# A state-space stage on five engines: the steps at which its side work is called, and the pattern by which two engines share a product

## The reference, cut to what matters

```python
xz = x @ W_in.T                                  # x is normalised ahead of this
xc, z = jnp.split(xz, 2, axis=-1)                # 512 channels each
xc = silu(causal_conv(xc, conv_w) + conv_b)      # 4 taps along the tokens
dBC = xc @ W_x.T                                 # 64 + 16 + 16 columns
delta = softplus(dBC[..., :64] @ W_dt.T + b_dt)
deltaA = jnp.exp(delta[..., None] * A)           # a decay for each channel and state
BX = delta[..., None] * Bm[:, :, None, :] * xc[..., None]
# h[l] = deltaA[l] * h[l-1] + BX[l], along the tokens, 16 states a channel
y = jnp.einsum('bldn,bln->bld', hs, Cm) + Dp * xc
out = y * silu(z) @ W_out.T                      # then x + out
```

## Time and profile before

| | us |
|---|---|
| three timed runs | 1959.77, 1966.07, 2140.01 |
| their median | 1966.07 |
| the profiled execution | 1966.89 |
| its span in the trace | 1965.2 |
| GpSimd busy in the span | 1076.1 (55%) |
| VectorE busy in the span | 1325.1 (67%) |
| TensorE, ScalarE busy in the span | 1295.3 (66%), 905.4 (46%) |

### The profile page before, as it was taken

One profiled execution on the slowest core, in us unless ns is written; L12 is line 12 of the kernel. 1 busy time (PEld: TensorE's weight loads), 2 busy tenths in 40 slices (PEclk: granted clock), 3 DMA queues, 4 the chain that ended last, 5 costly groups with the idle time before them and its releaser, 6 DMA issues. The chain is left out here.

```text
span 1965.2 us, 33999 instructions
## 1 busy us (share of the span) xinstructions
PE 1295.3 (66%) x14068; PEld 616.3 (31%) x14068; DVE 1325.1 (67%) x1605; ACT 905.4 (46%) x1622; POOL 1076.1 (55%) x463
## 2 busy tenths in 40 slices
PE   5384948577584849444687736567766766648875
PEld 2121313132222214121233412344444444433433
DVE  3699899999999898998610053778669767525102
ACT  4566575747475665643322134446345544213220
POOL 1899999999999999998200011442344245330000
PEclk9687969788686969666798867678788877668988
DMA  4928183654728282740899741212331222139997
GB/s 116 216 56 202 41 205 78 161 129 98 192 55 219 50 193 54 184 107 0 313 411 421 327 129 33 55 30 50 67 72 34 62 56 68 46 103 367 418 421 271
DMA packets 193706, 300.07 MB, mean 153 GB/s; under 512 B 82704, under 2 KB 125200, under 8 KB 177168
## 3 DMA queue, kind: packets, MB, share of 16 engines
q1 hardware_dynamic: 188512, 295.17, 49.9%
q10 hardware_dynamic: 4688, 2.19, 0.4%
q0 software_dynamic: 352, 0.52, 0.1%
HBM read 255.37 MB, written 42.47 MB: 152 GB/s over the span
## 5 line engine op out<-in xcount | busy, mean ns | idle before, releaser
L376 POOL TENSOR_TENSOR state<-dx_rep,b_rep 128x2048 f32<-128x2048 f32 x128 | 578.8, 4526 | 52.1 <-issue 21.3
L608 DVE TENSOR_TENSOR_SCAN psum<-psum,state 128x1024 f32<-128x1024 f32 x160 | 365.2, 2283 | 27.7 <-POOL state L376 14.5
L744 PE MATMUL psum<-state,sel 128*32 128x512 f32 x1024 | 188.4, 833 | 269.1 <-POOL state L385 251.6
L491 ACT ACTIVATE psum<-delta_rep,a_neg 128x511 f32<-128x511 f32 x512 | 330.8, 679 | 60.5 <-DVE state L608 60.3
L608 DVE TENSOR_TENSOR_SCAN state<-psum,state 128x1024 f32<-128x1024 f32 x96 | 218.8, 2279 | 34.1 <-ACT psum L491 34.1
L385 POOL TENSOR_TENSOR state<-state,c_rep 128x1024 f32<-128x1024 f32 x96 | 226.0, 2354 | 0.0
L615 DVE TENSOR_TENSOR state<-psum,c_rep 128x1024 f32<-128x1024 f32 x160 | 195.9, 1225 | 5.5
L744 PEld LDWEIGHTS psum<-state,sel 128*32 128x32 f32 x1024 | 28.9, 129 | 398.8 <-issue 320.2
L668 PE MATMUL psum<-xt,w_in 128*128 128x512 f32 x256 | 128.1, 647 | 38.2 <-ACT z_silu L458 25.8
L488 ACT COPY psum<-zeros 128x2 f32<-128x2 f32 x160 | 25.9, 162 | 236.1 <-DVE state L615 226.5
L1855 PE MATMUL psum<-xt_delta,w_qkv 128*128 128x512 f32 x192 | 107.2, 697 | 12.4 <-DVE attn_t L1669 11.2
(11 more groups left out here) (222 smaller groups left out, 2449.2 us busy)
## 6 DMA issues: line engine op xcount, KB each, us to landing
moe_w_set<-in_w SPq DMA_DIRECT2D x30, 4096.0 KB, 33.0
delta_rep<-delta_scratch SPq DMA_DIRECT2D x128, 256.0 KB, 5.5
dx_rep<-dx_scratch SPq DMA_DIRECT2D x128, 256.0 KB, 8.1
b_rep<-bc_scratch SPq DMA_DIRECT2D x32, 256.0 KB, 4.8
delta_scratch<-delta SPq DMA_DIRECT2D x32, 256.0 KB, 7.8
c_rep<-bc_scratch SPq DMA_DIRECT2D x32, 256.0 KB, 7.9
moe_x<-x_after SPq DMA_DIRECT2D x16, 512.0 KB, 8.8
moe_w_set<-in_w SPq DMA_DIRECT2D x4, 2048.0 KB, 31.5
```

The costliest lines, as they stand in the source:

```text
L376: nc.gpsimd.tensor_tensor(ring[q % RING][:, :, :], dx_rep[u % CHUNKS][:, :, :], free_bcast(b_rep[q // QPB % 2][:, g, :], 1, CB), ALU.mult) ...
L491: ins = nc.scalar.activation(dec[:, i, 1:], delta_rep[u % CHUNKS][:, c, 1:], ACT.Exp, scale=a_neg[:, dt * CB + c, g:g + 1])
L608: nc.vector.tensor_tensor_scan(bx if by_pool(k) else flat, flat, bx, 0.0, ALU.mult, ALU.add).then_inc(S["scan_done"], 1)
L744: ins = nc.tensor.matmul(bank[32 * c:32 * c + 32, :], sel[:, :], ring[q % RING][:, c, :], start=False, stop=(g == NG4 - 1), skip_group_che ...
```

## The change

The step numbers are taken out of the loops into four tables, and some get other values. On ScalarE the copies of the transposes go from step 5 to 6, those of the first two convolutions from 13 to 12, the padded copies of tiles 2 and 3 from 15 to 14, and the second pair of `z_silu` from 29 to 30. On VectorE the gate goes from 4 to 5 (of every 8), the statistics from 20 to 18, the shift from 25 to 24; the addition of the output, both halves at step 9 before, is made at step 7 (first half) and 8 (second half). TensorE calls the convolution of tile 0 right after the projections of tiles 0 and 1, one quad earlier; the projection of tile 1 waits for the second half of the addition, that of tile 0 for the first half alone. On GpSimd `delta_x` of tiles 0 and 1 goes from after quad 14 to after quad 12; tiles 2 and 3 stay after quad 15. Of an item's 16 odd halves GpSimd leaves those of quads 6, 8, 12 and 15 to VectorE, where it left 3, 7, 11 and 15. The lag of three quads is the same, and no instruction is added or taken away.

```diff
+    ACT_AT = dict(root=24, apply=27, xt=6, xp0=10, xp1=10, cc0=12, cc1=12, xp2=14, xp3=14, cc2=17, cc3=17, silu=18, z01=18, dbc=20, dl01=22, dl23=25, z23=30)
+    DVE_AT = dict(gate=5, ln=18, shift=24, add0=7, add1=8)
+    PE_AT = dict(turn=0, out=1, px0=2, px1=2, cv0=2, cv1=3, px2=4, px3=4, cv2=5, cv3=5, z01=6, dbc=7, dl01=8, dl23=10, z23=12)
+    POOL_AT = dict(lag=3, dx01=12, dx23=15, skip=(6, 8, 12, 15))
...
     def by_pool(k):
-        return k % 2 == 1 and (k // 2) % 4 != 3
+        return k % 2 == 1 and k // 2 % 16 not in POOL_AT["skip"]
...
-                    if q // QPB + 1 < B and q % QPB in (14, 15):
-                        for t in (0, 1) if q % QPB == 14 else (2, 3):
-                            delta_x(q // QPB + 1, t)
+                    for pair, slot in (((0, 1), "dx01"), ((2, 3), "dx23")):
+                        if q // QPB + 1 < B and q % QPB == POOL_AT[slot]:
+                            for t in pair:
+                                delta_x(q // QPB + 1, t)
...
-                def add_output(b):
+                def add_output(b, i):
                     dve.wait_ge(S["res_loaded"], 16 * (b + 1))
-                    for i in range(2):
-                        dve.wait_ge(S["out_psum"], 2 * b + i + 1)
-                        pair = x_res[:, 2 * i:2 * i + 2, :].rearrange("p s d -> p (s d)")
-                        nc.vector.tensor_tensor(pair, pair, mbank[i][:, :], ALU.add).then_inc(S["out_added"], 1)
+                    dve.wait_ge(S["out_psum"], 2 * b + i + 1)
+                    pair = x_res[:, 2 * i:2 * i + 2, :].rearrange("p s d -> p (s d)")
+                    nc.vector.tensor_tensor(pair, pair, mbank[i][:, :], ALU.add).then_inc(S["out_added"], 1)
...
-                    if i == 9 and n >= 2:
-                        add_output(n - 2)
+                    for side in range(2):
+                        if i == DVE_AT[f"add{side}"] and n >= 2:
+                            add_output(n - 2, side)
...
-                            pe.wait_ge(S["out_added"], 2 * (b - 1))
+                            pe.wait_ge(S["out_added"], 2 * (b - 2) + t + 1)
```

More of the change, by code:

```diff
@@ L523, in _ @@
                         norm_apply(1)
+                    at = ACT_AT
                     if n + 1 < B:
-                        if i == 24:
+                        if i == at["root"]:
                             norm_root(n + 1)
-                        if i == 27:
+                        if i == at["apply"]:
                             norm_apply(n + 1)
                     if n < B:
-                        if i == 5:
+                        if i == at["xt"]:
                             xt_copies(n)
[L532 to L544, removed]
+                        for t in range(DT):
+                            if i == at[f"xp{t}"]:
+                                xpad_copy(n, t)
+                        for t in range(DT):
+                            if i == at[f"cc{t}"]:
+                                conv_copy(n, t)
+                        if i == at["silu"]:
                             conv_silu(n)
+                        if i == at["z01"]:
                             z_silu(n, 0)
                             z_silu(n, 1)
+                        if i in (at["silu"], at["z01"]) and (i == at["z01"] or at["z01"] > at["silu"] + 1):
                             nc.scalar.preload_act_table_set("natural_log_exp_and_others")
-                        if i == 20:
+                        if i == at["dbc"]:
                             copy_dbc(n)
-                        if i == 22:
+                        if i == at["dl01"]:
                             step_sizes(n, (0, 1))
-                        if i == 25:
+                        if i == at["dl23"]:
                             step_sizes(n, (2, 3))
-                        if i == 29:
+                        if i == at["z23"]:
                             z_silu(n, 2)
@@ L641, in _ @@
                         norm_shift(1)
-                    if i % 8 == 4 and k >= 8:
+                    if i % 8 == DVE_AT["gate"] and k >= 8:
                         gate_y(k // 8 - 1)
                     if n + 1 < B:
-                        if i == 20:
+                        if i == DVE_AT["ln"]:
                             norm_statistics(n + 1)
-                        if i == 25:
+                        if i == DVE_AT["shift"]:
                             norm_shift(n + 1)
-                    if i == 9 and n >= 2:
-                        add_output(n - 2)
+                    for side in range(2):
+                        if i == DVE_AT[f"add{side}"] and n >= 2:
+                            add_output(n - 2, side)
                 gate_y(DT * B - 1)
-                add_output(B - 1)
+                add_output(B - 1, 0)
+                add_output(B - 1, 1)
             @block.tensor
```

39 lines of the change are left out of this document (17 added, 22 removed).

## The result

The median after is 1978.97 us (1970.42 to 1987.05, eight runs) against 1965.66 for the kernel before in the same runs. The ratio is 1.0073 [1.0047, 1.0099]: slower, where 1953 was forecast, and outside the range that was given. It lies within the 2% that the prediction gave 0.95. One of the eight runs of before, 2140.01 us, is in a slow state and is left out of the ratio.

The account below looks back on a forecast made before the run. GpSimd was taken as the bound, with VectorE nearly full. Terms -21.3 + 1.4 + 17.5 - 14.6 + 0.9 + 2.0 = -14.1 us against 1966.89 gave 1953 us, range 1947 to 1960 (chance 0.55).

Parts of the forecast that it names:

- the one on the shift: VectorE's norm shift at step 24: waits at most for GpSimd's running instruction, 0 to 4.5 us, out of spare time.
- The cover: VectorE's idle time, 8.8 us an item, was to hide its added waits and keep GpSimd's next input ahead.
- The third rival: VectorE becomes the bound if the shift waits out an input and other waits double: 1980, at worst 1995 us; chance 0.07.
- The prediction's own sign of being wrong: GpSimd waiting elsewhere, above all for the third to eighth sums, or VectorE no longer waiting for anything.
- Transfer waits: GpSimd's seven waits before an item's first input, for `delta_x` stored and loaded back, go: -21.3 us.
- The early `delta_x` on delta: GpSimd's product for tiles 0 and 1, after quad 12, waits briefly for delta: +1.4 us in seven items.
- `xt` on `project_z`: The second `delta_x` pair newly waits for TensorE's projection of tiles 2 and 3: 2.5 us seven times, +17.5.
- Sums in mid-item: GpSimd's waits on TensorE's sums: 14.6 of 17.7 us go, with 0.9 coming back in the first item.
- Last item: VectorE has no spare time there and waits for the output projection at the first addition: +2.0 us.
- The reading of the bound: GpSimd, the fuller of two nearly full engines, bounds; only its 4.9 us idle an item can be won.

Follow-up runs that it names:

- the four short stands: The changed kernel with the shift as four one-column VectorE instructions, each still with two SBUF tensors: 1974.63 us, ratio 1.0071 to the kernel before.
- the one-tensor shift: The changed kernel with the norm's shift as four VectorE instructions, each with one SBUF tensor and a per-partition scalar: 1945.99 us, ratio 0.9913 to before.
- with quad 11: The changed kernel with the one-tensor shift and quad 11 left to VectorE in place of quad 12: 1928.87 us, ratio 0.9826 to before.
- the two halves of the change tried alone: With the one-tensor shift: the changed kernel with GpSimd's old table, 1964.12 us; the kernel before with only GpSimd's new table, 1962.33 us.
- Taking the largest alone: The kernel before with the one-tensor shift and `delta_x` of tiles 0 and 1 after quad 12: 1971.83 us, ratio 1.0043.
- the probe: The kernel with quad 11 on VectorE plus an unused two-SBUF-tensor VectorE instruction four times an item: 2076.15 us in a single run.

## Why the prediction was wrong

**The step that failed** is the one on the shift: "it stood until GpSimd's instruction was through ... a whole input would cost 4.5, out of VectorE's spare time". Both halves of it were wrong, and because of the second the sum gave the shift no term at all. The place had been counted rightly for half of the items: in three the shift came 0.47 to 0.48 us ahead of the end of a product with C and went through there, as the earlier trace rows had suggested. In the other three it came 0.64, 1.04 and 1.17 us ahead of such an end, missed it, and stood through two more boundaries to GpSimd's next pause, for 11.9 to 12.4 us. The one row of before, 3.16 us, was read as "until the running instruction ends"; it was no evidence of an upper bound. There the shift got through at the boundary between the third input and the fourth, the first that it met.

The Trainium skill ("SBUF — State Buffer", section "Who interferes with whom") was used to make the same bound, by its rule that whoever starts first holds the port for the whole instruction. The runs agree that two SBUF inputs make VectorE stand behind GpSimd and that one does not (5.03 against 0.57 us); that the holder may go on from instruction to instruction, for 11.9 to 12.4 us here, they show beyond the rule, and the measurement decides.

**The cover was too large as well.** VectorE's 8.8 us idle an item were taken to hide a stand. Against 107.1 us an item without one, 12.2 us of stand cost 8.5 (115.6), 7.8 cost 5.3 (112.4), 5.0 cost 2.15 (109.3): about 2.5 to 3.7 us are hidden each time, not 8.8. The idle time of the whole item is no cover for a stand at its end; what counts is the slack up to the next thing that others wait for, and in after that is the gate, for which TensorE's output projection (7.42 us), the next sums and so GpSimd wait. With the four short stands, 1974.63, the range would have been missed too.

**The third rival** had the kind of it (VectorE late through the shift, slower than before), with 0.07. Its price was bounded by one input, 4.5 us, and its condition was that other waits double, which they needn't have done. The prediction's own sign of being wrong, that GpSimd waits elsewhere, came true, but at the item's second sum, where it had pointed at the third to eighth.

**The rest of the sum held**, and the kernel with the one-tensor shift shows it without the stand: -16.0 us at the end of the stage against -14.1. That it comes so near has some luck in it, since the terms miss by 1 to 2 us each, some up and some down.

- Transfer waits: -21.3, gone in after and with the one-tensor shift.
- The early `delta_x` on delta: 1.4 forecast, 0.6 in after, none in the list with one tensor.
- `xt` on `project_z`: +17.5 forecast, 18.0 and 18.8. It comes from the choice of quads: with quad 11 on VectorE it is zero.
- Sums in mid-item: -14.6 forecast; with one tensor one wait of 2.1 is left, in the first item, where 4.0 (3.1 and 0.9) were expected. In after the first item has 3.75 (2.82 and 0.93). The result was right and a part of the reason was not: with the additions at step 9 these waits are gone as well. The later asking, with GpSimd's product of quad 3 ahead, and the earlier convolution do it together, as the two halves of the change tried alone show.
- Last item: +2.0 forecast for the addition. From its first input to the MEMSET it is 120.0 us before (821.96 to 941.96), 124.5 in after (830.30 to 954.80) and 124.0 with one tensor. In the last of these VectorE waits 1.2 us at the first addition, where the term had 2.0; the rest is at the end of the item, which was not costed: 0.9 more at the last gate (2.06 against 1.19) and 1.7 more at the last output projection (5.60 against 3.88). That projection stretched because TensorE began it at the lower of its levels: the granted clock of its first 3 us is 0.50 with one tensor, and 1.00 before. Before, and with one tensor:

```profile
929.91 7.17 PE L727 MATMUL psum<-w_out,z_silu 128*128 128x256 f32 x32 [0.81 <-DVE z_silu L590]
```

```profile
912.16 8.90 PE L732 MATMUL psum<-w_out,z_silu 128*128 128x256 f32 x32 [0.81 <-DVE z_silu L594]
```

**The reading of the bound** was only half right. "Nothing but its 4.9 us can be won while it bounds" names a limit, and with quad 11 almost all of it was won: 109.4 to 104.6. But GpSimd's waits are not free to be taken one by one. Taking the largest alone made the kernel 0.4% slower, since GpSimd then waited 42.7 us for sums in place of 17.7. That it met a chain through VectorE, ScalarE and TensorE with a length of its own is the reading of those waits; no run joins that move with the other engines' steps alone.

## What to carry to other kernels

When GpSimd works without pauses, give no small VectorE instruction two SBUF tensors in a loop that others wait on: a scalar for each partition does the same work (0.57 us for four here) and did not stand in any run. An operation's longest duration in its group, beside its shortest, finds such stands, which no list of waits shows. And idle time hides a delay only as far as the next result that another engine needs: measure from the delay's place to there, not over the loop.

## What was not expected of the hardware

In all traces here a standing VectorE instruction with two SBUF tensors got through at the first boundary between two GpSimd instructions that it met, or, once it had missed that one, only when GpSimd paused: after 11.9 to 12.4 us in after, 7.5 to 8.2 with the shift at step 25, 8.1 and 13.8 in the probe, whatever boundaries went by meanwhile. What makes it catch or miss the first one stays open. It is not the lead alone: 0.47 us ahead of a product's end was caught and 0.64 missed in after, 0.26 ahead of an input's end was missed in the probe, and 0.27 to 0.30 ahead of one, with the shift at step 25, was caught. Leads of 1.45 and 2.3 us were caught too. The seven long ones of the probe agree within 0.05 us, so the same place seems to give the same outcome. In the changed kernel long and short alternate; that a long stand, which makes the item 9 us longer, moves the next shift to the place that catches would explain it, and was not tested.
